# TensorE goes tile by tile instead of quad by quad: 8 units of scores, the products of the next tile, 8 blocks of rows, with one s_t buffer and score copies in twos by two engines

## The chip, the core and the metric

One Trainium2 chip; the kernel runs on one of its cores. The time is the device time of one execution in microseconds (us). Before the change it is 617.23 us (median of 3 runs, 616.33 to 617.63).

## The reference

```python
def _L0_rec_ref(F, W, K_w, Q_w):            # F (2048, 64, 128), W (64, 64, 128), K_w and Q_w (128, 128)
    Kf = jnp.einsum('bjd,ed->bje', F, K_w)
    S = jnp.einsum('bid,bjd->bij', F, Kf)   # 64 x 64 scores of each batch
    out = jnp.einsum('bij,ijd->bid', S, W)  # row i of every batch times W[i]
    out = out + jnp.einsum('bid,ed->bie', F, Q_w)
    return out
```

All in float32.

## The kernel before, in words

**Tiles, units, quads.** The 2048 batches are 16 tiles of 128. A tile is 8 units of 16 batches, a quad is 4 units, so there are 32 quads. TensorE does three kinds of work:

- *Products* (`three`, L377 to L379): F times K_w and F times Q_w, both with F transposed (128 values of d on the partitions). For accuracy F and each weight are split in a high and a low part, and a product is three matmuls with a moving operand of 512 columns (hi by hi, lo by hi, hi by lo) into one PSUM bank. A chunk is 512 columns, half a unit: one K product and one Q product, 6 matmuls. A quad has 8 chunks, 48 matmuls.
- *Scores* (`scores`, L460): for each batch a full float32 matmul with a stationary operand of 64 columns (`kf`) and a moving one of 64 (F from `f_ring`), 16 for a unit. The even and the odd batch of a pair go to the lower and the upper 64 partitions of the output, so they lie in different column halves of the array.
- *Rows* (`rows_out`, L493): for each row i of the reference a float32 matmul of W[i] (64 x 128, stationary) and the scores of that row for all 128 batches of a tile (moving, 128 columns). Row m and row 32 + m lie in different row halves of the array. A block is 4 + 4 rows, 8 matmuls, in two banks; a tile has 8 blocks, and four of them are done in each quad.

A float32 matmul of scores or rows shows in the trace as two weight loads and two matmuls, so a quad has 128 records of scores and 64 of rows.

**The other engines.** ScalarE (ACT) copies every K product out of PSUM to `kf` (`copy_kf`, L180) and every Q product to `q_out` (`copy_q`, L190), and makes the high part `f_hi` of each unit (`split_f`, L175). VectorE (DVE) makes the low part `f_lo` (L289), copies the scores of each unit from PSUM to `s_t` in three copies (`copy_s`, L315 to L317), and adds `q_out` to each block of rows (`sum_out`, L328) into one of 4 buffers of `o_sb`. SyncE (SP) issues the loads of F (1 MB for two units, into a ring of 4 such pairs) and the stores of a block (512 KB).

**Order.** Everything is written out by hand, and engines meet by semaphores. TensorE does for each quad g: the scores of g (`scores_quad`), four blocks of rows of quad r = g - 2 (`rows_quad`), the products of g + 1 (`project`). The first two quads have no rows (`project_early`), the last part is `end`. `s_t` has two buffers, one for each parity of the tile. PSUM has 8 banks; tables (STEADY, EARLY, SCORES, ROWS, END_...) say which bank is used for what, and TensorE waits before each reuse until the bank was read: for `kf_copied` and `q_copied`, `s_copied`, or `out_done`. `f_hi` and `f_lo` have a place for each of 4 units. At the start the first 8 chunks come as own loads, the first of them in two halves.

## Time and profile before

| | us |
|---|---|
| median of 3 runs | 617.23 |
| the profiled execution | 617.93 |
| its span, first to last instruction | 616.1 |
| TensorE matmuls busy | 604.9 (98%) |
| TensorE weight loads busy | 527.4 (86%) |
| VectorE busy | 460.1 (75%) |
| ScalarE busy | 391.3 (64%) |

The granted TensorE clock is 0.997 of full speed over the span. Busy times are unions of overlapping instructions, so a busy matmul row does not tell how fast the matmuls follow one another; the start times in the timeline do. The profile's page names lines of this kernel; after the change the same work has other line numbers.

### The profile page before, as it was taken

The numbers are of one execution on the slowest core, as the hardware profiler recorded it, in microseconds if no ns is written. First come the engines' busy times: TensorE is split into PE (matmuls) and PEld (weight loads), VectorE is DVE, ScalarE is ACT, GpSimd is POOL, SyncE is SP. The second block draws the span as 40 slices with busy tenths as digits, with TensorE's granted clock in tenths as the row PEclk, the third lists the DMA queues.
The fourth block names the chain that finished last, engine by engine and source line by source line (L and its number), as shares of the span: only waits on it lengthen the run. The fifth ranks groups of instructions, "written<-read, shape, count | busy, mean of one in ns | idle before, by whom it ended". The sixth has DMA issues, their size and how long they took to land.

```text
span 616.1 us, 17320 instructions
## 1 busy us (share of the span) xinstructions
PE 604.9 (98%) x7691; PEld 527.4 (86%) x7691; DVE 460.1 (75%) x647; ACT 391.3 (64%) x649; POOL 0.2 (0%) x4
## 2 busy tenths in 40 slices
PE   8999999999999999999999999999999999999994
PEld 6888888888888888888888888888888888888884
DVE  5668777787777887777887778877778777788756
ACT  7786577655677555676556775556765567765550
POOL 0000000000000000000000000000000000000000
PEclk9999999999999999999999999999999999999998
DMA  7646455775555775557755557655567655577247
GB/s 279 262 152 249 178 208 193 269 271 195 203 203 227 273 260 184 192 198 266 274 211 189 206 218 273 260 187 194 202 257 274 233 172 215 204 274 263 97 171 293
DMA packets 29161, 137.55 MB, mean 223 GB/s; under 512 B 3232, under 2 KB 3744, under 8 KB 21024
## 3 DMA queue, kind: packets, MB, share of 16 engines
q1 hardware_dynamic: 28800, 136.33, 60.0%
q8 instruction: 60, 0.98, 0.6%
q10 hardware_dynamic: 288, 0.13, 0.1%
q14 instruction: 13, 0.11, 0.0%
HBM read 69.34 MB, written 67.11 MB: 221 GB/s over the span
## 4 chain that ended last, share of the span: by engine, by line
PE 94%; DVE 3%; issue 1%; DMA 1%; ACT 1%; SPq 0%; DVEq 0%
PE ps L377 20%; PE ps L460 19%; PE ps L379 19%; PE ps L378 19%; PE ps L493 18%; DVE o_sb L328 2%; DMA f_ring<-f 1%; DVE s_t L315 0%; DVE s_t L317 0%; ACT f_hi L175 0%; DVE s_t L316 0%; DVE f_lo L289 0%; ACT q_out L190 0%; SPq L123 0%; ACT kf L180 0%
## 5 line engine op out<-in xcount | busy, mean ns | idle before, releaser
L180 ACT ACTIVATE kf<-ps 128x512 f32<-128x512 f32 x256 | 160.1, 625 | 192.9 <-PE ps L379 188.7
L289 DVE TENSOR_TENSOR f_lo<-f_ring,f_hi 128x1024 fp32r<-128x1024 f32 x124 | 146.2, 1218 | 53.3 <-ACT f_hi L175 53.2
L190 ACT ACTIVATE q_out<-ps 128x512 f32<-128x512 f32 x256 | 159.5, 628 | 5.5
L328 DVE TENSOR_TENSOR o_sb<-ps,q_out 128x1024 f32<-128x1024 f32 x128 | 150.3, 1218 | 10.3 <-PE ps L493 8.5
L460 PEld LDWEIGHTS ps<-f_ring,kf 128*64 128x64 f32 x4096 | 122.0, 138 | 11.0 <-issue 10.9
L175 ACT ACTIVATE f_hi<-f_ring 128x1024 fp32r<-128x1024 f32 x122 | 128.4, 1095 | 2.0
L460 PE MATMUL ps<-f_ring,kf 128*64 128x64 f32 x4096 | 126.5, 223 | 0.0
L493 PE MATMUL ps<-s_t,w_sb 64*128 64x128 f32 x2048 | 122.9, 275 | 1.5 <-DVE s_t L317 1.3
L493 PEld LDWEIGHTS ps<-s_t,w_sb 64*128 64x128 f32 x2048 | 116.8, 188 | 4.1 <-DVE s_t L317 1.4
L315 DVE COPY s_t<-ps 128x256 f32<-128x256 f32 x126 | 53.1, 422 | 78.5 <-PE ps L460 76.4
L377 PE MATMUL ps<-f_hi,k_hi 128*128 128x512 f32 (+1 forms) x257 | 103.5, 403 | 1.2 <-DVE f_lo L277 1.2
L379 PE MATMUL ps<-f_hi,k_lo 128*128 128x512 f32 (+1 forms) x257 | 100.2, 390 | 0.0
L378 PE MATMUL ps<-f_lo,k_hi 128*128 128x512 f32 (+1 forms) x257 | 100.0, 389 | 0.0
L377 PE MATMUL ps<-f_hi,q_hi 128*128 128x512 f32 x256 | 99.9, 390 | 0.0
L379 PE MATMUL ps<-f_hi,q_lo 128*128 128x512 f32 x256 | 99.7, 389 | 0.0
L378 PE MATMUL ps<-f_lo,q_hi 128*128 128x512 f32 x256 | 99.6, 389 | 0.0
L377 PEld LDWEIGHTS ps<-f_hi,k_hi 128*128 128x128 f32 x257 | 48.3, 188 | 14.1 <-DVE f_lo L277 1.6
L379 PEld LDWEIGHTS ps<-f_hi,k_lo 128*128 128x128 f32 x257 | 48.2, 188 | 10.3
L378 PEld LDWEIGHTS ps<-f_lo,q_hi 128*128 128x128 f32 x256 | 48.1, 188 | 10.3
L379 PEld LDWEIGHTS ps<-f_hi,q_lo 128*128 128x128 f32 x256 | 48.0, 188 | 10.4
L377 PEld LDWEIGHTS ps<-f_hi,q_hi 128*128 128x128 f32 x256 | 48.0, 188 | 10.2
L378 PEld LDWEIGHTS ps<-f_lo,k_hi 128*128 128x128 f32 x257 | 48.3, 188 | 8.8
(23 smaller groups left out, 129.7 us busy)
## 6 DMA issues: line engine op xcount, KB each, us to landing
out<-o_sb SPq DMA_DIRECT2D x128, 512.0 KB, 5.3
f_ring<-f_t SPq DMA_DIRECT2D x62, 1024.0 KB, 6.9
w_sb<-w SPq DMA_DIRECT2D x1, 2048.0 KB, 11.8
f_ring<-f SPq DMA_DIRECT2D x7, 256.0 KB, 5.2
f_ring<-f SPq DMA_DIRECT2D x2, 128.0 KB, 2.4
k_raw<-k_t ACTq DMA_DIRECT2D x1, 64.0 KB, 2.4
q_raw<-q_t ACTq DMA_DIRECT2D x1, 64.0 KB, 3.1
```

Of the source, the lines that this page charges most:

```text
L175: nc.scalar.activation(f_hi[:, e, :], f_unit(v), COPY).then_inc(fhi_done, 1)
L180: nc.scalar.activation(kf[:, c // 2, c % 2 * CK:(c % 2 + 1) * CK, :, :].rearrange("d k h i -> d (k h i)"), ps[:, product_bank(g, 2 * c), : ...
L190: nc.scalar.activation(q_out[:, t % 2, :, :].rearrange("d i (h b) -> d i h b", h=2)[:, :, :, at:at + CK], ps[:, product_bank(g, 2 * c + 1) ...
L289: nc.vector.tensor_tensor(f_lo[:, e, :], f_unit(v), f_hi[:, e, :].bitcast(F32), ALU.subtract).then_inc(flo_done, 1)
L315: nc.vector.tensor_copy(s_t[:, parity, :, same], src[:, 0, :, :])
L328: nc.vector.tensor_tensor(o_sb[:, n % OBUF, :, :], ps[:, bank:bank + 2, :], q_out[:, parity, :, :].rearrange("d (s m) b -> d s (m b)", s=2 ...
L377: nc.tensor.matmul(dst, w_hi[:, :], hi, start=True, stop=False)
L378: nc.tensor.matmul(dst, w_hi[:, :], lo, start=False, stop=False)
L379: return nc.tensor.matmul(dst, w_lo[:, :], hi, start=False, stop=True)
L460: ins = nc.tensor.matmul(ps[h * N:(h + 1) * N, score_bank(g, e), k * N:(k + 1) * N], kf[:, e, k, h, :], rows, start=True, stop=True)
L493: ins = nc.tensor.matmul(ps[:, row_bank(r, e) + s, x * P:(x + 1) * P], w_sb[half, m, :], cols, start=True, stop=True)
```

## The change

TensorE's order is by tile: the scores of tile t (8 units in 8 banks, unit e in bank e), the products of tile t + 1 (16 chunks), the 8 blocks of rows of tile t. `s_t` has one buffer, `kf` has places for 8 units, `f_hi` and `f_lo` for 3, the ring of F for 6 pairs of units. Scores leave PSUM in pairs of units (copies of 512 values for each partition instead of 256), pairs 0 and 2 by VectorE, pairs 1 and 3 by ScalarE. VectorE also makes `f_hi` of three units in a tile (`both_f`) and does its 8 sums in a row. The rows of the last tile are done in two parts (`rows_last`, `sum_last`): part 0 for the batches of units 0 to 3, part 1 for units 4 to 7, each with a moving operand of 64 columns and all 64 weights. At the start the first unit comes in four half chunks, one of them issued by ScalarE, and W is loaded right after the first 12 units of F.

```diff
-RING = 2 * UNITS // QUAD
+RING = 6
+SPLIT = 3
-        s_t = sbuf("s_t", [P, 2, HALF, P])
+        s_t = sbuf("s_t", [P, HALF, P])
...
+        def scores_of(p):
+            return ps[:, 2 * p:2 * p + 2, :].rearrange("p e (k s m) -> p s m (e k)", k=KP, s=2)
...
         @block.sync
             load_half(0)
-            load_half(1)
-            for c in range(1, CHUNKS):
+            load_half(2)
+            load_half(3)
+            for c in range(2, PIECES):
                 load_first(c)
-            load_f(2)
-            load_f(3)
...
+            for p in range(2, RING):
+                load_f(p)
+            sp.dma_start(w_sb[:, :, :].rearrange("j m d -> j (m d)"), w).then_inc(w_in, 16)
+            for t in range(TILES):
+                if t >= 1:
+                    for k in range(4, 7):
+                        store(t - 1, k)
+                load_next(t, 0)
+                if t >= 1:
+                    store(t - 1, 7)
+                for j in range(1, PAIRS):
+                    load_next(t, j)
+                for k in range(4):
+                    store(t, k)
...
         @block.scalar
+            for t in range(1, TILES):
+                copy_s(t - 1, 1)
+                copy_s(t - 1, 3)
+                for c in range(CHUNKS):
+                    copy_kf(t, c)
+                    copy_q(t, c)
+                    if c % 4 == 1:
+                        split_f(t * UNITS + 3 + c // 2)
+                split_f((t + 1) * UNITS + 2)
...
         @block.vector
+            def copy_s(t, p):
+                dve.wait_ge(s_done, t * UNITS + 2 * p + 2)
+                src, same, cross = scores_of(p), same_cols(p), cross_cols(p)
+                nc.vector.tensor_copy(s_t[:, :, same], src[:, 0, :, :])
+                nc.vector.tensor_copy(s_t[upper, :, cross], src[lower, 1, :, :])
+                nc.vector.tensor_copy(s_t[lower, :, cross], src[upper, 1, :, :]).then_inc(s_copied, 1)
...
+            for t in range(TILES):
+                v = (t + 1) * UNITS
+                copy_s(t, 0)
+                low_f(v + 2)
+                copy_s(t, 2)
+                low_f(v + 3)
+                both_f(v + 4)
+                low_f(v + 5)
+                both_f(v + 6)
+                low_f(v + 7)
+                both_f(v + 8)
+                low_f(v + 9)
+                if t < TILES - 1:
+                    for k in range(UNITS):
+                        sum_out(t, k)
+            for half in range(2):
+                for k in range(4):
+                    sum_last(half, k)
...
         @block.tensor
+            def project(t):
...
+                    if c >= 4:
+                        pe.wait_ge(kf_copied, n - 3)
+                    elif t >= 1:
+                        pe.wait_ge(s_copied_act if c % 2 else s_copied, (t - 1) * 2 + c // 2 + 1)
...
+            def scores_tile(t):
+                for e in range(UNITS):
...
+                    elif e % 2 == 0:
+                        pe.wait_ge(out_done, (t - 1) * UNITS + 5 + e // 2)
+                    scores(t, e)
+            def rows_tile(t):
+                if t == 0:
+                    pe.wait_ge(w_in, 16)
+                for k in range(UNITS):
+                    if k < 4:
+                        pe.wait_ge(kf_copied, (t + 1) * CHUNKS + 13 + k)
+                        pe.wait_ge(q_copied, (t + 1) * CHUNKS + 13 + k)
+                    else:
+                        pe.wait_ge(out_done, t * UNITS + k - 3)
+                    row_block(t, k)
+            def rows_last(part):
+                t = TILES - 1
+                for k in range(4):
...
+                    for x in range(2 * IR):
+                        m = k * 2 * IR + x
+                        for s in range(2):
+                            half = slice(s * N, (s + 1) * N)
+                            cols = s_t[half, m, :].rearrange("p (h b) -> p h b", h=2)[
+                                :, :, part * KP * 4:(part + 1) * KP * 4]
...
+                            ins = nc.tensor.matmul(ps[:, bank + s, x * N:(x + 1) * N], w_sb[half, m, :], cols,
+                                                   start=True, stop=True)
...
-            for g in range(QUADS - 1):
-                scores_quad(g)
...
-                if g >= 2:
-                    rows_quad(g)
-                    project(g + 1)
...
+            project(0)
+            for t in range(TILES):
+                scores_tile(t)
+                if t < TILES - 1:
+                    project(t + 1)
+                    rows_tile(t)
+            for part in range(2):
+                rows_last(part)
```

TensorE in the middle of the program before: the last products of a quad (L378, L379), the scores of the next (L460), rows of an earlier one (L493), the next products.

```order
L378 MATMUL ps<-f_lo,q_hi 128x512
L379 MATMUL ps<-f_hi,q_lo 128x512
L460 MATMUL ps<-f_ring,kf 64x64 x64
L493 MATMUL ps<-s_t,w_sb 128x128 x32
L377 MATMUL ps<-f_hi,k_hi 128x512
L378 MATMUL ps<-f_lo,k_hi 128x512
```

TensorE in the middle of the program now: the last products of tile t + 1 (L388, L389), the rows of tile t (L466), the scores of tile t + 1 (L440), the next products.

```order
L388 MATMUL ps<-f_lo,q_hi 128x512
L389 MATMUL ps<-f_hi,q_lo 128x512
L466 MATMUL ps<-s_t,w_sb 128x128 x64
L440 MATMUL ps<-f_ring,kf 64x64 x128
L387 MATMUL ps<-f_hi,k_hi 128x512
L388 MATMUL ps<-f_lo,k_hi 128x512
```

Runs of one kind are twice as long, and rows stand ahead of scores.

VectorE over one quad before: four score copies of three instructions each (L315 to L317), the four sums (L328) from the third on, four low parts (L289).

```order
L317 COPY s_t<-ps 64x32x8
L328 TENSOR_TENSOR o_sb<-ps,q_out 128x1024 [waits o_stored0,o_done]
L315 COPY s_t<-ps 128x32x8 [waits s_done]
L316 COPY s_t<-ps 64x32x8
L317 COPY s_t<-ps 64x32x8
L328 TENSOR_TENSOR o_sb<-ps,q_out 128x1024 [waits o_stored1,o_done]
L328 TENSOR_TENSOR o_sb<-ps,q_out 128x1024 [waits o_stored2,o_done]
L328 TENSOR_TENSOR o_sb<-ps,q_out 128x1024 [waits o_stored3,o_done]
L289 TENSOR_TENSOR f_lo<-f_ring,f_hi 128x1024 [waits fhi_done] x4
```

VectorE now, from the last low part of a tile (L292) over its eight sums (L325) to the first score copy of the next tile (L314 to L316).

```order
L292 TENSOR_TENSOR f_lo<-f_ring,f_hi 128x1024 [waits fhi_done]
L325 TENSOR_TENSOR o_sb<-ps,q_out 128x1024 [waits o_stored0,q_copied,o_done]
L325 TENSOR_TENSOR o_sb<-ps,q_out 128x1024 [waits o_stored1,o_done]
L325 TENSOR_TENSOR o_sb<-ps,q_out 128x1024 [waits o_stored2,o_done]
L325 TENSOR_TENSOR o_sb<-ps,q_out 128x1024 [waits o_stored3,o_done]
L325 TENSOR_TENSOR o_sb<-ps,q_out 128x1024 [waits o_stored0,o_done]
L325 TENSOR_TENSOR o_sb<-ps,q_out 128x1024 [waits o_stored1,o_done]
L325 TENSOR_TENSOR o_sb<-ps,q_out 128x1024 [waits o_stored2,o_done]
L325 TENSOR_TENSOR o_sb<-ps,q_out 128x1024 [waits o_stored3,o_done]
L314 COPY s_t<-ps 128x32x16 [waits s_done]
L315 COPY s_t<-ps 64x32x16
L316 COPY s_t<-ps 64x32x16
```

The sums now stand eight in a row, so the fifth waits for the store of the first of the same row of sums (o_stored0), where before a sum waited for a store of the quad before.

TensorE at the end of the program before (rows, the last four units of scores, eight blocks of rows of 128 columns):

```order
L493 MATMUL ps<-s_t,w_sb 128x128 x32
L460 MATMUL ps<-f_ring,kf 64x64 x64
L493 MATMUL ps<-s_t,w_sb 128x128 x64
```

And now (eight blocks of rows, the last eight units of scores, `rows_last`):

```order
L466 MATMUL ps<-s_t,w_sb 128x128 x64
L440 MATMUL ps<-f_ring,kf 64x64 x128
L504 MATMUL ps<-s_t,w_sb 128x64 x128
```

The last rows are 128 matmuls of 64 columns where they were 64 of 128.

## Rows read from the trace of the kernel before

**Rows 1.** The page: busy time (share of the span) and instructions of each engine.

```profile
PE 604.9 (98%) x7691; PEld 527.4 (86%) x7691; DVE 460.1 (75%) x647; ACT 391.3 (64%) x649; POOL 0.2 (0%) x4
```

**Rows 2.** TensorE's longest wait after the start: total us, times, longest.

```profile
PE ps L493 <- DVE s_t L317: 1.3, 1, 1.3
```

**Rows 3.** Timeline of PE, 318 to 338: start, us, engine, line, operation, count.

```profile
318.49 0.50 PE L377 MATMUL ps<-f_hi,k_hi 128*128 128x512 f32 x1
...
321.37 0.39 PE L377 MATMUL ps<-f_hi,k_hi 128*128 128x512 f32 x1
...
329.30 0.39 PE L379 MATMUL ps<-f_hi,q_lo 128*128 128x512 f32 x1
329.62 3.95 PE L460 MATMUL ps<-f_ring,kf 128*64 128x64 f32 x128
333.50 3.84 PE L493 MATMUL ps<-s_t,w_sb 64*128 64x128 f32 x64
337.27 0.50 PE L377 MATMUL ps<-f_hi,k_hi 128*128 128x512 f32 x1
```

**Rows 4.** Costliest groups: records | busy us, mean ns of one | idle before, releaser.

```profile
L460 PEld LDWEIGHTS ps<-f_ring,kf 128*64 128x64 f32 x4096 | 122.0, 138 | 11.0 <-issue 10.9
L493 PEld LDWEIGHTS ps<-s_t,w_sb 64*128 64x128 f32 x2048 | 116.8, 188 | 4.1 <-DVE s_t L317 1.4
```

**Rows 5.** Timeline of the end, all engines, from 592 on.

```profile
592.54 1.83 PE L493 MATMUL ps<-s_t,w_sb 64*128 64x128 f32 x28
...
593.75 1.22 DVE L328 TENSOR_TENSOR o_sb<-ps,q_out 128x1024 f32<-128x1024 f32 x1 [6.60 <-PE ps L493]
...
596.31 3.81 PEld L460 LDWEIGHTS ps<-f_ring,kf 128*64 128x64 f32 x128
596.31 3.95 PE L460 MATMUL ps<-f_ring,kf 128*64 128x64 f32 x128
...
598.28 0.41 DVE L315 COPY s_t<-ps 128x256 f32<-128x256 f32 x1
...
601.57 7.42 PE L493 MATMUL ps<-s_t,w_sb 64*128 64x128 f32 x128 [1.31 <-DVE s_t L317]
602.77 9.14 DVE L328 TENSOR_TENSOR o_sb<-ps,q_out 128x1024 f32<-128x1024 f32 x8 [1.88 <-PE ps L493]
```

**Rows 6.** Stores: the median to landing of those issued from 604.0, 611.9, 339 (two).

```profile
out<-o_sb SPq DMA_DIRECT2D x1, 512.0 KB, 2.6
out<-o_sb SPq DMA_DIRECT2D x1, 512.0 KB, 3.8
out<-o_sb SPq DMA_DIRECT2D x2, 512.0 KB, 4.7
```

**Rows 7.** The page: DMA issues: count, size, median us from issue to landing.

```profile
f_ring<-f_t SPq DMA_DIRECT2D x62, 1024.0 KB, 6.9
```

**Rows 8.** Timeline of ACT, from 325 on.

```profile
325.60 1.09 ACT L175 ACTIVATE f_hi<-f_ring 128x1024 fp32r<-128x1024 f32 x1
326.55 0.62 ACT L190 ACTIVATE q_out<-ps 128x512 f32<-128x512 f32 x1
327.02 0.64 ACT L180 ACTIVATE kf<-ps 128x512 f32<-128x512 f32 x1
```

**Rows 9.** Timeline of the start, all engines.

```profile
5.02 0.28 PE L377 MATMUL ps<-f_hi,k_hi 128*128 128x256 f32 x1
...
5.73 0.40 PE L377 MATMUL ps<-f_hi,q_hi 128*128 128x512 f32 x1
...
6.33 0.63 ACT L165 ACTIVATE f_hi<-f_ring 128x512 fp32r<-128x512 f32 x1 [1.71 <-DMA f_ring<-f]
...
7.60 0.42 DVE L283 CAST f_hi<-f_ring 128x512 fp32r<-128x512 f32 x1
...
7.74 0.50 PE L377 MATMUL ps<-f_hi,k_hi 128*128 128x512 f32 x1 [1.15 <-DVE f_lo L277]
```

More of the change, by code:

```diff
@@ L25 @@
 CK = BANK // (2 * N)
-CHUNKS = QUAD * TOK // BANK
-RING = 2 * UNITS // QUAD
+CHUNKS = UNITS * TOK // BANK
+FIRST = 4
+PIECES = FIRST * TOK // BANK
+PAIRS = UNITS // 2
+RING = 6
+SPLIT = 3
 OBUF = 4
 WARM = 8
-STEADY = (2, 3, 6, 7, 0, 1, 4, 5)
-EARLY = (6, 7, 4, 5, 0, 1, 2, 3)
-SCORES = (0, 1, 2, 3)
-ROWS = (4, 6, 0, 4)
-END_SCORES = (2, 3, 6, 7)
-END_AHEAD = (2, 6, 0, 4)
-END_ROWS = (0, 4, 2, 6)
+BOTH = [v for v in range(FIRST, TILES * UNITS) if v in (4, 5) or v >= UNITS and v % UNITS in (0, 4, 6)]
 def build(nc, f_0, f_t, k_t, q_t, w, out):
@@ L74, in build @@
         ps = psum("ps", [P, 8, BANK])
-        f_half = [sem(f"f_half{n}") for n in range(2)]
-        f_first = [sem(f"f_first{n}") for n in range(CHUNKS)]
+        f_half = [sem(f"f_half{n}") for n in range(4)]
+        f_first = [sem(f"f_first{n}") for n in range(PIECES)]
         f_in = [sem(f"f_in{n}") for n in range(RING)]
@@ new lines, in _ @@
+            sp.dma_start(w_sb[:, :, :].rearrange("j m d -> j (m d)"), w).then_inc(w_in, 16)
[10 more added lines that the diff above has]
+                    store(t, k)
+            for k in range(4, UNITS):
+                store(TILES - 1, k)
@@ L319, in sum_out, with low_f, both_f @@
-            def sum_out(r, e):
-                n = r * QUAD + e
-                u = n % UNITS
-                parity = n // UNITS % 2
+            def low_f(v):
+                if v >= TILES * UNITS:
+                    return
+                dve.wait_ge(fhi_done, sum(1 for x in range(FIRST, v + 1) if x not in BOTH))
+                low_unit(v)
+            def both_f(v):
+                if v >= TILES * UNITS:
+                    return
+                dve.wait_ge(f_in[v // 2 % RING], 16 * f_loads(v))
+                dve.wait_ge(q_done, 2 * (v - SPLIT) + 2)
+                nc.vector.tensor_copy(f_hi[:, v % SPLIT, :], f_unit(v)).then_inc(fhi_dve, 1)
+                dve.wait_ge(fhi_dve, 3 + sum(1 for x in BOTH if x <= v))
+                low_unit(v)
@@ L397, in project_first @@
                 ins.then_inc(k_done, 1)
-                pe.wait_ge(qlo_done, 1)
-                q_product(0, 0)
-                for c in range(1, CHUNKS):
-                    pe.wait_ge(flo_first, c + 2)
+            def project(t):
+                for c in range(CHUNKS):
+                    n = t * CHUNKS + c
+                    if n < 2:
+                        k_halves(n)
+                        if n == 0:
+                            pe.wait_ge(qlo_done, 1)
+                        q_product(n)
+                        continue
+                    if n < PIECES:
+                        pe.wait_ge(flo_first, n + 3)
+                    elif n % 2 == 0:
+                        pe.wait_ge(flo_done, n // 2 - FIRST + 1)
@@ L451, in scores @@
-            def scores(g, e):
-                v = g * QUAD + e
+                        pe.wait_ge(q_copied, n - 3)
+                    q_product(n)
+            def scores(t, e):
+                v = t * UNITS + e
                 for k in range(KP):
```

403 lines of the change are left out of this document (136 added, 267 removed).

## The prediction

> **What bounds the kernel now.** I read the page first: TensorE's matmuls are busy for 604.9 of 616.1 us and no other engine is above 75% [rows 1]. Then the list of waits: TensorE has almost none, the longest after the start is 1.3 us near the end [rows 2]. So time can only come out of the pace at which TensorE's own instructions follow one another, and the timeline of one quad shows that [rows 3]: products from 318.49, scores from 329.62, rows from 333.50, the next products from 337.27. That is 11.13 + 3.88 + 3.77 = 18.78 us a quad.
>
> I compare each phase with its inner pace. Products: from 321.37 to 329.30 are 35 steps, 0.2266 us each, so 48 need 10.88; the phase takes 0.25 more. Scores: a matmul is a couple of records. The 128 weight loads of a run are busy for 3.81 us [rows 5], the last of them for 0.14 [rows 4], so 63 steps from couple to couple take 3.67, 0.0583 each; 64 need 3.73, the phase takes 0.15 more. Rows: doubling a run from 64 to 128 records adds 7.42 - 3.84 = 3.58 us busy for 32 couples [rows 3, 5], 0.1119 each; the phase takes 3.77, 0.19 more than 3.58. So each quad pays 0.25 + 0.15 + 0.19 = 0.59 us for changing from one kind to the next three times.
>
> **The change part by part.** *Longer runs.* A tile has one run of each kind: scores 3.88 + 64 x 0.0583 = 7.61, products 11.13 + 10.88 = 22.01, rows 3.77 + 3.58 = 7.35, together 36.97 us, against 2 x 18.78 = 37.56. That is 0.59 less for each of 15 tiles, 8.8 us, if TensorE never waits. No matmul is added up to the last tile.
>
> *Does it wait? The sums.* I count from the start of a tile's scores: products from 7.6, rows from 29.63, next scores at 36.97. The first sum starts 1.21 after the rows (592.54 to 593.75 [rows 5]), at 30.84; eight in a row take 9.14, 1.13 from one to the next and about 1.22 for each [rows 5]. Blocks of rows come every 0.89, so the sums fall behind. Block 4 of rows (33.3) needs sum 0, over at 32.1; block 7 (36.0) needs sum 3, over at 35.5; the scores of units 0 and 1 (36.97) need sum 4, over at 36.6; units 2, 4 and 6 (38.8, 40.7, 42.6) need the sums that end at 37.7, 38.8 and 40.0. No wait, but only 0.4 to spare at two places. The sums have to start on time: the last low part on VectorE before them depends on ScalarE's split after chunk 13 (28.6) and ends at about 29.8, 1.0 early.
>
> *The stores.* There are 4 output buffers, so sum 4 (35.4) waits for store 0, issued at 32.1. A store without other traffic lands in 2.6 us, the eighth of eight in a row in 3.8 [rows 6]: 34.7. Sum 7 (38.8) needs store 3, about 38.6. SP issues the loads of F in between: the first stands behind the stores of blocks 4 to 6 and goes out at 2.3 instead of 2.1, the last at 7.8. At a median of 6.9 us to landing [rows 7] they are over long before 32, so I take the values without traffic. Stores issued some us after two loads took 4.7 [rows 6]. The F that the first load brings is split from 13.4 on, 11 us after its issue.
>
> *Score copies.* A copy of 512 values from PSUM is in no row. Bounds: 0.42 (256 values [rows 5]) and 1.13 (the sum of 1024 [rows 5]); on the line between, 0.66. VectorE's copy of pair 0 goes from 3.0 to 5.0, a low part to 6.1, pair 2 to 8.1. The products' chunk 0 wants pair 0 at 7.6 and chunk 2 wants pair 2 at 10.4. With 1.13 a copy they end at 6.4 and 10.9: 0.5 late. ScalarE takes 0.47 for 512 values and 0.95 for 1024 in a row [rows 8], so pair 3 goes from 7.8 to 9.3 and the first kf copy (ready at 8.6) starts 0.7 late. A product comes every 0.68, ScalarE wins 0.2 on each and loses 0.95 with a split; TensorE allows it four chunks, 5.4 us. Hidden.
>
> *Three places for f_hi and f_lo.* Unit v + 3 of a tile can be split when the products of unit v are done (10.7). ScalarE splits it after two copies, 11.2 to 12.2, the low part (1.13) is there at 13.5, and TensorE wants it at 15.9: 2.4 to spare. Units v + 5 and v + 7 repeat this; v + 4 and v + 6, both parts by VectorE, have 3. VectorE's work in a tile gets less: 6 copies of 0.66 for 24 of 0.42, plus three high parts of about 0.7 (estimated from the copies).
>
> *The start.* TensorE waits from 6.42 to 7.74 for chunk 1, whose 256 KB ScalarE gets at 6.33 [rows 9]. As two halves, the first issued earlier, it should be there about one microsecond sooner, but chunk 2 is no earlier: VectorE got it at 7.60 [rows 9], and TensorE now asks for its split at 7.8. Bounds of the waiting that is left: 0 and 1.3; I take 0.5. Then scores start at 5.02 + 2 x (0.71 + 0.68) + 14 x 1.36 + 0.09 + 0.5 = 27.4 (0.71 is a K product in halves, 5.02 to 5.73).
>
> *The last rows.* `rows_last` has 128 matmuls of 64 columns where 64 of 128 did, with twice the weight loads. Is a couple of rows paced by its moving columns or by its weights? Rows (128 stationary, 128 moving) take 0.1119, scores (64 and 64) 0.0583: both explain that. The weight-load records are 188 ns for 128 stationary columns and 138 for 64 [rows 4]: 50 ns for 64 columns, so the streaming part for 128 is at least 100 ns, all of the pace of rows. I therefore take 0.1119 for a couple also with 64 moving columns: 128 x 0.1119 = 14.32 us. The lower bound is 128 x 0.0583 = 7.5; above 14.3 there is none, since two loads of that width already pass in that time together with twice the moving columns.
>
> The Trainium skill ("TensorE: Matmul & The Clock Gate", section LDWEIGHTS) says that a weight load takes its columns divided by 1.2 ns, whatever the rows: an estimate of 107 ns for 128 columns. The same page's section on the back-to-back gap has a rule by moving columns alone. By the first rule the last rows would take 13.7 us, by the second they would be at the lower bound; the slope of the weight-load rows agrees with the first. It speaks against this part of the change.
>
> **The sum.** Scores of tile 0 at 27.4; plus 15 x 36.97 = 554.6 gives 582.0 for the scores of the last tile, plus 7.6 gives 589.6 for the last rows (their score copies come in time: pairs 0 and 1 by 5.9, pair 3 at 9.3, before block 3). Last sum: 14.32 + 0.32 later (0.32 is 1.21 less 8 couples), 604.3; 1.21 for it, 0.03 to issue, 2.6 to land, and 0.4 from the last landing to the end as before (611.9 + 3.8 to 616.1 [rows 6]): 608.5. That is 7.6 under the span of 616.1, so 610.3 for an execution like the profiled one (617.9), and 617.2 - 7.6 = **609.6 us** for the median.
>
> **Rivals.** *A, the forecast*: last rows at the pace of weights, no wait in the tiles, 609.6.
>
> *B, last rows at the pace of moving columns.* Then the eight sums bound the end: 589.6 + 0.93 + 0.32 + 7 x 1.13 + 1.21 + 0.03 + 3.8 + 0.4 = 604.2, 4.3 less: 605.3. For it: scores with 64 moving columns do run at half the time. Against it: they have half the stationary columns too.
>
> *C, small waits in each tile*, where 0.4 is to spare: a sum chain or a PSUM copy later than I walked it. At 0.3 for each of 15 tiles, 4.5 more: 614.1. For it: two margins of 0.4, and no row for the 512 copy. Against it: the paces are steady to hundredths.
>
> *D, slower: sums wait for stores.* If a store lands in 4.7 us, as after loads [rows 6], store 0 lands at 36.8, sum 4 ends at 38.0 and TensorE waits 1.0 before units 0 and 1: 15 x 1.0 = 15 more, 625. It decides from the landing of store 0: above 3.7 us TensorE waits, above 4.2 the 0.5 a tile that was to be gained is gone. Against it: no load is issued within 24 us ahead.
>
> *E, the change doesn't do what it says*: the 0.59 is not paid for changing kind, but comes for each 4 units, as from instruction supply. Then a tile still takes 37.56, 8.8 more: 618.4. Against it: inside a run the steps are even.
>
> **Chances.** A 0.57, B 0.17, C 0.15, D 0.07, E 0.04. A measurement of this kernel can tell about 0.2% (1.2 us) from no change. Faster: A, B and most of C, 0.88; within 0.2%: 0.04, out of C; slower: D, most of E, 0.08. The range takes in B and most of C: 604.6 to 614.3, with D, E and the worse part of C left out.
>
> **What would show it.** In the profile after: scores, products and rows of a tile at 7.61, 22.01 and 7.35 us with a period of 36.97; if a phase is longer, the list of waits names sum, copy or store. Couples of the last rows 0.11 apart (A) or 0.06 (B). Sum 4 of each tile with no idle time ahead (not D). TensorE's wait for chunk 1 under 0.5 us. I am wrong if TensorE shows waits in each tile, or if the gap at a change of kind grows with the length of the run.

## The result and the profile after

The kernel after takes 621.12 us (median of 6 runs, 618.88 to 623.89), against 617.19 for the kernel before, timed beside it (6 runs): 1.0065 times as long, with a 95% interval of 1.0049 to 1.0082. The forecast was 609.6 with a range to 614.3: wrong in sign. The profiled execution took 620.9 us, its span is 619.1, and the granted TensorE clock is 0.995 of full speed over the span.

The page of the kernel after: busy engines, the queue of instructions, and the issues of stores and loads with their median to landing (these answer to [rows 1] and [rows 7]):

```profile
PE 606.5 (98%) x7822; PEld 535.9 (87%) x7822; DVE 403.9 (65%) x411; ACT 402.0 (65%) x695; POOL 0.2 (0%) x4
...
q8 instruction: 62, 1.02, 0.6%
...
out<-o_sb SPq DMA_DIRECT2D x128, 512.0 KB, 4.4
f_ring<-f_t SPq DMA_DIRECT2D x62, 1024.0 KB, 10.5
```

Two things are new. A load lands in 10.5 us where it took 6.9 [rows 7]. And there is a queue that I had not looked at: the engines' own instructions come by DMA during the run, in 62 packets, 1.02 MB in all, 16 KB each.

Next the timeline of TensorE's matmuls over one tile (start, us, engine, line, operation, count):

```profile
139.14 7.68 PE L440 MATMUL ps<-f_ring,kf 128*64 128x64 f32 x256
146.75 0.50 PE L387 MATMUL ps<-f_hi,k_hi 128*128 128x512 f32 x1
...
168.76 7.42 PE L466 MATMUL ps<-s_t,w_sb 64*128 64x128 f32 x128
176.10 0.57 PE L440 MATMUL ps<-f_ring,kf 128*64 128x64 f32 x12
```

Scores 7.61, products 22.01, rows 7.34, a tile 36.96: what was forecast, to a hundredth. Other tiles are longer. The list of waits (engine, line, releaser: total, times, longest) has them, where [rows 2] had one of 1.3 us:

```profile
DVE o_sb L325 <- DMA out<-o_sb: 11.1, 10, 1.8
...
PEld ps L388 <- issue: 2.9, 1, 2.9
...
PEld ps L440 <- issue: 2.3, 5, 0.6
...
PEld ps L387 <- issue: 2.1, 1, 2.1
...
PEld ps L440 <- DVE o_sb L325: 0.9, 3, 0.4
```

The rows named PEld are TensorE's weight loads; the matmul behind a late load waits with it. Most of TensorE's new waits end with "issue": no engine and no data transfer of the program released it. Timeline of matmuls at the longest:

```profile
258.89 0.39 PE L388 MATMUL ps<-f_lo,q_hi 128*128 128x512 f32 x1
259.12 0.39 PE L389 MATMUL ps<-f_hi,q_lo 128*128 128x512 f32 x1
262.23 0.39 PE L387 MATMUL ps<-f_hi,k_hi 128*128 128x512 f32 x1 [2.72 <-issue]
```

And the same stretch by windows (busy time of each engine, then granted clock, DMA share, GB/s): the DMA engines are full all the while.

```profile
259.00:260.00 1.00, 0.51 (x3) 0.27 (x2) 0.00 (x0) 0.96 (x3) 0.00 (x0) 1.00 0.98 385
260.00:261.00 1.00, 0.00 (x0) 0.00 (x0) 0.00 (x0) 0.88 (x2) 0.00 (x0) 1.00 1.06 434
261.00:262.00 1.00, 0.00 (x0) 0.00 (x0) 0.00 (x0) 0.00 (x0) 0.00 (x0) 1.00 0.99 414
```

Among those transfers, between 259.75 and 260.8, is one packet of the queue of instructions:

```profile
q8 instruction: 1, 0.02, 5.6%
```

The second long wait, matmuls again:

```profile
448.64 0.40 PE L387 MATMUL ps<-f_hi,k_hi 128*128 128x512 f32 x1
448.88 0.39 PE L388 MATMUL ps<-f_lo,k_hi 128*128 128x512 f32 x1
451.14 0.39 PE L389 MATMUL ps<-f_hi,k_lo 128*128 128x512 f32 x1 [1.87 <-issue]
...
452.66 0.63 PE L389 MATMUL ps<-f_hi,k_lo 128*128 128x512 f32 x1
...
455.22 0.63 PE L389 MATMUL ps<-f_hi,k_lo 128*128 128x512 f32 x1
455.65 0.46 PE L387 MATMUL ps<-f_hi,q_hi 128*128 128x512 f32 x1
```

This one settles what kind of wait it is. It lies inside one product, between the lo by hi and the hi by lo matmul, where the code has no semaphore at all. It costs 2.0 us. From 1.2 us after its end on, steps of 0.43 in place of 0.23 follow, 1.6 us more.

Where the 10.6 us go that lie between forecast and trace at the end (608.5 and 619.1): I took the start times of all matmuls and subtracted the steady steps. After the first score:

| what | us |
|---|---|
| eight waits ended by "issue": 0.40, 0.42, 0.06, 2.88, 0.65, 0.16, 2.03, 0.61 | 7.2 |
| the slow steps after the wait at 448.88 | 1.6 |
| four small waits at the first or second unit of scores of a tile (0.15 to 0.25) | 0.8 |
| steps of under 0.05 each | 0.7 |
| start (27.24 for 27.4) and end (27.0 from the last scores for 26.5) | 0.3 |

All eight waits of the first line come at the same place in TensorE's stream: counting all its instructions in the trace (weight loads, matmuls and the 198 semaphore and drain instructions among them, 15,842 in all), 193 or 194 past a multiple of 256. And 62 packets of 16 KB for 15,842 instructions are 64 bytes each, 256 to a packet. So the waits lie where a new block of instructions begins.

The packets confirm it. Packet n (the first is 0) can be laid beside instruction 256(n + 1) + 193. At the eight waits TensorE goes on 1.20 to 1.54 us after that packet has landed: the one from 259.79 to 260.72 stands ahead of the restart at 262.23, the one from 448.93 to 449.89 ahead of 451.14. In the kernel before, laid out in the same way, every packet lands at least 2.7 us ahead of its place.

The end, answering to [rows 5]: last rows, weight loads and matmuls.

```profile
599.73 14.37 PEld L504 LDWEIGHTS ps<-s_t,w_sb 64*128 64x128 f32 x256
599.73 14.51 PE L504 MATMUL ps<-s_t,w_sb 64*128 64x64 f32 x256
```

### The profile page after: what moved, and what is told of

Read it like the earlier page. It is cut to its first block, busy times and chain, and to the rows that moved or that the text cites. A ratio compares the mean times of both kernels' runs of the same rounds, so it can differ in the third digit from the quotient of the medians.

```text
span 619.1 us, 17442 instructions
## 1 busy us (share of the span) xinstructions
PE 606.5 (98%) x7822; PEld 535.9 (87%) x7822; DVE 403.9 (65%) x411; ACT 402.0 (65%) x695; POOL 0.2 (0%) x4
## 3 DMA queue, kind: packets, MB, share of 16 engines
q8 instruction: 62, 1.02, 0.6%
## 4 chain that ended last, share of the span: by engine, by line
PE 94%; DMA 2%; DVE 1%; issue 1%; ACT 0%; DVEq 0%
PE ps L440 20%; PE ps L387 19%; PE ps L389 19%; PE ps L388 19%; PE ps L466 15%; PE ps L504 2%; DMA out<-o_sb 2%; DVE o_sb L325 1%; PE ps L511 1%; DVE o_sb L338 0%; ACT s_t L219 0%; ACT s_t L217 0%; DVE zeros L345 0%; ACT s_t L218 0%; DVEq L91 0%
## 5 line engine op out<-in xcount | busy, mean ns | idle before, releaser
L292 DVE TENSOR_TENSOR f_lo<-f_ring,f_hi 128x1024 fp32r<-128x1024 f32 x124 | 151.8, 1224 | 163.5 <-ACT f_hi L194 161.9
L208 ACT ACTIVATE q_out<-ps 128x512 f32<-128x512 f32 x256 | 156.7, 612 | 7.5 <-PE ps L389 0.3
L325 DVE TENSOR_TENSOR o_sb<-ps,q_out 128x1024 f32<-128x1024 f32 x120 | 140.2, 1219 | 32.5 <-PE ps L466 20.7
L199 ACT ACTIVATE kf<-ps 128x512 f32<-128x512 f32 x256 | 155.6, 608 | 7.8 <-PE ps L389 4.3
L217 ACT ACTIVATE s_t<-ps 128x512 f32<-128x512 f32 x32 | 19.1, 598 | 180.7 <-PE ps L440 180.7
L440 PE MATMUL ps<-f_ring,kf 128*64 128x64 f32 x4096 | 125.0, 223 | 1.7 <-issue 1.4
L440 PEld LDWEIGHTS ps<-f_ring,kf 128*64 128x64 f32 x4096 | 121.8, 138 | 5.0 <-issue 2.3
L466 PEld LDWEIGHTS ps<-s_t,w_sb 64*128 64x128 f32 x1920 | 108.4, 188 | 5.3 <-issue 5.3
L466 PE MATMUL ps<-s_t,w_sb 64*128 64x128 f32 x1920 | 111.2, 274 | 0.0
L387 PE MATMUL ps<-f_hi,k_hi 128*128 128x512 f32 (+1 forms) x258 | 102.0, 395 | 2.7 <-issue 2.7
L389 PE MATMUL ps<-f_hi,k_lo 128*128 128x512 f32 (+1 forms) x258 | 100.5, 390 | 1.9 <-issue 1.9
L388 PE MATMUL ps<-f_lo,k_hi 128*128 128x512 f32 (+1 forms) x258 | 100.5, 389 | 0.0
L389 PE MATMUL ps<-f_hi,q_lo 128*128 128x512 f32 x256 | 99.9, 390 | 0.0
L388 PE MATMUL ps<-f_lo,q_hi 128*128 128x512 f32 x256 | 99.9, 390 | 0.0
L194 ACT ACTIVATE f_hi<-f_ring 128x1024 fp32r<-128x1024 f32 x77 | 82.0, 1064 | 0.0
L388 PEld LDWEIGHTS ps<-f_lo,k_hi 128*128 128x128 f32 x258 | 48.7, 189 | 12.5 <-issue 2.9
L387 PEld LDWEIGHTS ps<-f_hi,k_hi 128*128 128x128 f32 x258 | 48.7, 189 | 10.6
L389 PEld LDWEIGHTS ps<-f_hi,k_lo 128*128 128x128 f32 x258 | 48.6, 189 | 10.1
L388 PEld LDWEIGHTS ps<-f_lo,q_hi 128*128 128x128 f32 x256 | 48.3, 189 | 10.1
L389 PEld LDWEIGHTS ps<-f_hi,q_lo 128*128 128x128 f32 x256 | 48.2, 188 | 10.2
## 6 DMA issues: line engine op xcount, KB each, us to landing
f_ring<-f_t SPq DMA_DIRECT2D x62, 1024.0 KB, 10.5
```

Source lines behind the costliest of these rows:

```text
L194: nc.scalar.activation(f_hi[:, v % SPLIT, :], f_unit(v), COPY).then_inc(fhi_done, 1)
L199: nc.scalar.activation(kf[:, c // 2, c % 2 * CK:(c % 2 + 1) * CK, :, :].rearrange("d k h i -> d (k h i)"), ps[:, 2 * c % 8, :], COPY).then ...
L208: nc.scalar.activation(q_out[:, t % 2, :, :].rearrange("d i (h b) -> d i h b", h=2)[:, :, :, at:at + CK], ps[:, (2 * c + 1) % 8, :].rearra ...
L217: nc.scalar.activation(s_t[:, :, same], src[:, 0, :, :], COPY)
L292: nc.vector.tensor_tensor(f_lo[:, v % SPLIT, :], f_unit(v), f_hi[:, v % SPLIT, :].bitcast(F32), ALU.subtract).then_inc(flo_done, 1)
L325: nc.vector.tensor_tensor(o_sb[:, n % OBUF, :, :], ps[:, bank:bank + 2, :], q_out[:, t % 2, :, :].rearrange("d (s m) b -> d s (m b)", s=2) ...
```

## The experiments

The theory (F in some of the expectations): TensorE's next block of instructions comes late, because its DMA runs behind data that the DMA engines already have. A block lasts 3.8 us in scores (512 records take 7.61) and 7.3 in rows, but a load takes about 10 us to land. The rivals: the sums and their stores hold TensorE up; or the waits belong to the work at that place; or long fast stretches need instructions faster than they come, whatever the data traffic (L in the first expectations; in that of late_stores, L says that the four loads alone are enough).

| kernel | median us (lowest to highest, runs) | ratio to before (95%) | span of the profile |
|---|---|---|---|
| light_loads | 616.73 (614.60 to 619.17, 10) | 0.9982 (0.9968 to 0.9997) | 615.2 |
| light_stores | 612.68 (612.60 to 613.36, 4) | 0.9925 (0.9909 to 0.9942) | 610.9 |
| spaced_loads | 616.81 (615.66 to 617.85, 10) | 0.9986 (0.9976 to 0.9995) | 615.7 |
| wide_end | 620.77 (618.41 to 624.68, 7) | 1.0068 (1.0037 to 1.0100) | 617.2 |
| quiet_scores | 613.71 (613.45 to 613.99, 5) | 0.9936 (0.9923 to 0.9948) | 611.9 |
| quiet_wide | 612.06 (611.07 to 613.45, 5) | 0.9912 (0.9898 to 0.9927) | 611.6 |
| shifted | 624.75 (1) | | 622.9 |
| before_traffic | 621.93 (621.55 to 622.94, 4) | 1.0074 (1.0059 to 1.0090) | 619.8 |
| late_stores | 622.37 (617.99 to 628.08, 10) | 1.0059 (1.0034 to 1.0084) | 626.3 |
| quiet_buf5 | 611.81 (611.36 to 614.16, 6) | 0.9916 (0.9904 to 0.9929) | 609.6 |
| split_loads | 618.83 (616.29 to 621.40, 10) | 1.0018 (1.0002 to 1.0034) | 617.4 |
| split_both | 664.47 (664.08 to 665.94, 4) | 1.0766 (1.0750 to 1.0782) | 663.0 |

**light_loads.** All loads of F after the first six pairs bring an eighth of the bytes; the rest of each pair keeps old values, and the instructions stay.

```diff
-                             f_t[p, :, :]).then_inc(f_in[p % RING], 16)
+                cols = 2 * TOK if p < RING else 2 * TOK // 8
+                ... f_t[p, :, :cols]).then_inc(f_in[p % RING], 16)
```

> The changed kernel, but after the first 12 units each load of F brings only 256 of its 2048 columns (128 KB instead of 1 MB), so later products and scores use old F. Theory F (TensorE's program comes by DMA in blocks of 256 instructions, and a block is late when the DMA engines have a backlog of loads and stores while scores and rows use up a block in 3.8 us): the gaps inside scores and products at positions 193 or 194 modulo 256 of TensorE's instructions vanish, every tile takes 36.97 us, the time is 609 to 611 us. Theory L (the run of rows and scores, now 768 instructions in 15 us, outruns the supply of instructions by itself, whatever the data traffic): the gaps stay, 619 to 622 us.

616.73: below the kernel after and hardly below before, between what F (609 to 611) and L (619 to 622) asked. The two long waits and the slow steps are gone. Short ones stay, in the middle of scores, in its list of waits:

```profile
PEld ps L441 <- issue: 3.0, 7, 0.7
```

So the long waits need the full loads, and the short ones don't; loads alone are not the whole cause.

**light_stores.** Each store writes 64 KB in place of 512; the rest of the output is not written.

```diff
-                sp.dma_start(out[t, k, :, :], ...
+                sp.dma_start(out[t, k, :, :IR * P // 4], ...[:, :IR * P // 4] ...
```

> The changed kernel, but each store writes only 256 of the 1024 columns of its block (128 KB instead of 512 KB). Theory F: the stores are the backlog at the beginning of the scores, so most gaps at the block boundaries go; those behind the burst of four loads (late in the scores, early in the products) may stay; no sum waits for a store; 609 to 615 us. Theory L: the gaps stay and only the sums' waits of about 1 us in all go, 618 to 621 us.

612.68. (The edit writes 64 KB a store, not the 128 of the expectation.) The first two tiles of its trace take 1.1 us more each, with a wait at a block boundary in either; from the third on a tile takes 36.97, but for one that takes 0.6 and one that takes 0.1 more. The loads are untouched, and nearly all later waits are gone, the long ones too. Each cure removes more than its own part, as if it counted how much data is in line when the block of instructions is asked for; late_stores, below, shows that this is not the whole of it.

**spaced_loads.** All bytes, but load j of a tile also waits for a K product (2j + 1) of the next tile, so the four loads are spread over the products.

```diff
                     sp.wait_ge(s_done, t * UNITS + 2 * j + 2)
+                    sp.wait_ge(k_done, (t + 1) * CHUNKS + 2 * j + 1)
```

> The changed kernel, complete, but SP issues the four loads of F of a tile one by one during the products: load j waits in addition for the K product of chunk 2j of the next tile, so no load is under way during rows and scores. Theory F: nearly no gaps at block boundaries, 609 to 613 us; the F of the first load lands about 1 to 2 us before its split, so no new wait for F. Theory L: 619 to 622 us. If F comes late instead, VectorE and then TensorE wait in the products at unit 4 of each tile, some 0.5 us a tile more.

616.81, as light_loads, and again between F (609 to 613) and L (619 to 622): no long wait, but some 3 us of short ones in the scores, where the stores still are.

**quiet_scores.** SyncE issues the four loads and the stores of blocks 4 to 7 only during the products, in turn, so that nothing is issued while scores run. Same instructions on all other engines.

```diff
-                    for k in range(4, 7): store(t - 1, k)
-                load_next(t, 0)
-                ...
+                for j in range(PAIRS):
+                    in_products(t, 3 * j)          # waits k_done
+                    load_next(t, j)
+                    if t >= 1:
+                        in_products(t, 3 * j + 2)
+                        store(t - 1, 4 + j)
```

> The changed kernel, complete, with another order on SP alone: during the products of a tile, paced by waits for K products of chunks 0 to 11, it issues load 0, store 4, load 1, store 5, load 2, store 6, load 3, store 7; stores 0 to 3 go out as before. So nothing but the rest of stores 0 to 3 is under way during the scores. Theory F (late instruction blocks, because of the backlog of data DMAs): the gaps at 193 and 194 modulo 256 in scores and early products go, and as loads and stores no longer meet, no sum waits for a store: tiles at 36.97 us, 609.5 to 611.5 us. Theory L (the long run by itself): 616 us or more, as with spaced loads.

613.71: 7.4 us under the kernel after with the same work and the same bytes. At the block boundaries 0.12 us of waiting is left in the trace after the first tile. This is the clearest run: TensorE's long fast stretch does no harm by itself. It is still 2 us over what F asked (609.5 to 611.5): the expectation had no sum waiting for a store, and its trace has 2.0 us of TensorE waiting for such sums.

**late_stores.** Only the stores of blocks 4 to 7 go into the products; the loads stay in the scores.

```diff
+                for j in range(PAIRS): load_next(t, j)
+                for k in range(4, UNITS):
+                    sp.wait_ge(k_done, (t + 1) * CHUNKS + 3 * k - 9)
+                    store(t - 1, k)
```

> The kernel after, with one edit: SyncE issues the stores of blocks 4 to 7 of the tile before not in the first microseconds of the scores but one by one during the products (after 3, 6, 9 and 12 K products). The four loads are issued at their old places, during the scores. Theory S (TensorE's next instructions come late only where a backlog of data transfers and a long fast stretch meet; the stores of the tile before are the first half of that backlog, as light_stores had it with lighter stores): the waits of 0.2 to 0.8 us in the middle of the scores go, the two large waits in the early products go as well or stay single, span 611 to 612.5, median 612.5 to 614. Rival L (the burst of four loads alone is enough for the large waits): the two waits of 2 to 3 us near 259 and 449 us, with the slow clock behind one of them, stay or come at other tiles, span 615 or more. Rival N (instruction supply has nothing to do with it): as the kernel after, 619 to 621.

622.37, no better than the kernel after: theory S there fell, rival L held. The profile is of the longest of its ten runs, so I take places from it and no totals. TensorE in one tile (scores begin at 178.76):

```profile
181.27 4.53 PE L439 MATMUL ps<-f_ring,kf 128*64 128x64 f32 x147 [0.42 <-DVE o_sb L324]
187.70 1.50 PE L439 MATMUL ps<-f_ring,kf 128*64 128x64 f32 x44 [1.91 <-issue]
```

DMA queues of that kernel from 178.8 to 185.1 (packets, MB, share): only data.

```profile
q1 hardware_dynamic: 291, 1.64, 69.8%
issues: line engine op xcount, KB each, median us to landing
f_ring<-f_t SPq DMA_DIRECT2D x2, 1024.0 KB, 5.6
```

And from 185.1 to 187.6: the block of instructions, just ahead of TensorE's restart.

```profile
q8 instruction: 1, 0.02, 2.2%
```

In light_stores, where the first load was issued at nearly the same point of the scores (2.3 us into them, here 2.1), the block of this tile (scores from 178.08) came at 181.3 to 182.4, in a stretch in which the DMA engines had moments of rest, and the scores ran through:

```profile
178.08 7.68 PE L441 MATMUL ps<-f_ring,kf 128*64 128x64 f32 x256
...
185.70 0.50 PE L388 MATMUL ps<-f_hi,k_hi 128*128 128x512 f32 x1
```

```profile
q8 instruction: 1, 0.02, 5.3%
```

The block is either just ahead of the loads or behind them. That heavier stores push the block before it back, and so this one behind the loads, fits both traces, but it is argued, not shown. The spread of this kernel (10 us over ten runs) would go with such a race.

**before_traffic.** The reverse, in the kernel before: one more load of 1 MB for each quad, into a spare buffer that nobody reads, issued after the first unit of scores.

```diff
+                if g < QUADS:
+                    sp.wait_ge(s_done, g * QUAD + 1)
+                    sp.dma_start(spare[:, :], f_t[g, :, :]).then_inc(spare_in, 16)
```

> The kernel before, with one more load of 1 MB in each quad into a spare place that nobody reads, issued when the first unit of scores is done, ahead of the two loads of F. Theory F: the kernel before too gets gaps at one residue modulo 256, in scores, rows or the first products, and takes 619 to 630 us; its sums may wait for stores as well. Theory L: its runs are short, so no such gaps, at most waits of sums, 617 to 619 us.

621.93, slower by what theory F in its bare form would ask, but not for its reason. The quads keep their pace, as in [rows 3]:

```profile
328.83 3.95 PE L467 MATMUL ps<-f_ring,kf 128*64 128x64 f32 x128
332.72 3.84 PE L500 MATMUL ps<-s_t,w_sb 64*128 64x128 f32 x64
336.49 0.50 PE L384 MATMUL ps<-f_hi,k_hi 128*128 128x512 f32 x1
```

317.71 to 336.49 is 18.78. The loss is at the end. SyncE issues the last added load ahead of four stores, so these go out from 597.10 on, where before it was 595.00, and take 9.8 us to land, where it was 4.7; a sum waits for the first of them, and TensorE for the sum:

```profile
DVE o_sb L335 <- DMA out<-o_sb: 4.4, 1, 4.4
PEld ps L500 <- DVE o_sb L335: 3.3, 3, 1.5
```

Its packets of instructions all land at least 3.1 us ahead of their places. So traffic does no harm either with short fast stretches (scores and rows of a quad are 384 records in 7.65 us, between products that need 11.1 us for 96). With quiet_scores this says that both are needed: a long stretch (768 records in 15 us) and data in line.

**shifted.** Are the waits tied to the block or to the work at that place? 32 small matmuls ahead of the first product (64 records) move all block boundaries against the work.

```diff
+            for n in range(32):
+                nc.tensor.matmul(ps[:, 0, :N], zeros[:, :P], zeros[:, :N], start=True, stop=True)
             pe.wait_ge(klo_done, 1)
```

> The changed kernel with 32 more small matmuls of zeros (64 records of TensorE) ahead of the first product, about 2 us. If late blocks of 256 instructions cause the gaps (F), they stay at the same residue, 193 or 194 modulo 256 counted over all of TensorE's records, and so move to other places of the work: the gap inside the scores of a tile moves 32 couples earlier. If they belong to a place of the work (a wait for another engine), they stay at the same couple of the same tiles and their residue moves by 64. 617 to 626 us.

In the kernel after the third tile (scores from 101.67) waits at 106.33, 4.66 us into them. Now:

```profile
110.32 7.68 PE L440 MATMUL ps<-f_ring,kf 128*64 128x64 f32 x255
119.09 0.27 PE L440 MATMUL ps<-f_ring,kf 128*64 128x64 f32 x1 [1.09 <-issue]
```

The wait is after record 510 of 512. 64 records are 0.95 us of scores, so the old boundary is now at 3.7 and the next, 3.8 on, at 7.5: there. All of its "issue" waits at scores and products are again at 193 or 194 of 256. They belong to the block. In this trace and the ten others of the kernel after and its variants but split_both, each of the 45 steps of over 0.3 us at such a place ends 1.2 to 1.6 us after a packet of instructions has landed. (My expectation took a batch of scores for two records; it is four, with its weight loads.) The single time of 624.75 is no price of the waits: the 32 matmuls took 6.9 us and not 2, the lower clock was granted until 17.2 us where it was 5.2, and the first scores start at 36.2 for 27.2. From there to its last scores this trace is 5.4 us shorter than that of the kernel after.

**wide_end.** The last rows as the tiles have them: 64 matmuls of 128 columns.

```diff
-            for part in range(2):
-                rows_last(part)
+            pe.wait_ge(s_copied, TILES * 2)
+            pe.wait_ge(s_copied_act, TILES * 2)
+            rows_tile(TILES - 1)
```

> The changed kernel, but the rows of the last tile are done as those of all others, 64 matmuls of 128 columns, after all score copies, and not in two parts. If the last rows are paced by their weight loads (theory W: 128 x 0.112 us with 64 columns), the rows start 1.8 us later, take 7.2 instead of 14.5 us, and eight sums at 1.13 us bound the end: 24 us from the last scores to the end instead of 27, so 2.5 to 3.5 us less than the changed kernel, near 618 us. If the end was bound by something else, no difference.

Matmuls, then VectorE, of its end (last scores from 591.45):

```profile
601.19 7.42 PE L462 MATMUL ps<-s_t,w_sb 64*128 64x128 f32 x128 [1.99 <-ACT s_t L219]
```

```profile
602.39 7.15 DVE L325 TENSOR_TENSOR o_sb<-ps,q_out 128x1024 f32<-128x1024 f32 x6 [1.84 <-PE ps L462]
610.77 2.46 DVE L325 TENSOR_TENSOR o_sb<-ps,q_out 128x1024 f32<-128x1024 f32 x2 [1.23 <-DMA out<-o_sb]
```

Half the records take half the time: 14.51 / 256 and 7.42 / 128 are 0.057 and 0.058 us each, with 64 columns moving and with 128. The pace is that of the weights. But only 1.2 of the 7.1 us come through (25.8 from last scores to the end, against 27.0): the rows start 2.1 later, since they want all score copies, and the sums then wait for stores. The median is not told from that of the kernel after, and the 618 expected did not come.

**quiet_wide.** quiet_scores and wide_end together.

> As quiet_scores, and the rows of the last tile as 64 matmuls of 128 columns. By theory F 1.2 us less than quiet_scores (the tail with wide rows took 25.8 us from the last scores against 27.0): 608.5 to 610.5 us. By theory L near 615 us.

612.06: faster than both kernels, but 1.6 us over the range expected. What is left in its trace over 36.97 a tile is 2.1 us, 1.8 of it at the first or second unit of scores. The wide end gave nothing in it: from the last scores to the end it took 26.8 us, in quiet_scores 26.7. TensorE waits 2.0 us for the last score copy, then the granted clock is at the lower level from 595.6 to 599.0, and the last rows take 9.04 us where wide_end had 7.42.

**quiet_buf5.** One more buffer of sums, 5 in place of 4. The raw weights share its place until its first use, and 19 warm-up matmuls of 216 columns stand for 8 of 512.

```diff
-OBUF = 4
+OBUF = 5
...
+        k_raw = o_sb[:, OBUF - 1, 1, :D]
+        q_raw = o_sb[:, OBUF - 1, 1, D:2 * D]
```

> quiet_wide with one more buffer for the sums: 5 places of o_sb in place of 4 (to make room, the raw weights lie in the fifth place until its first use, and the warm-up matmuls have 216 columns in place of 512, 19 of them in place of 8). The sum of block 4 then no longer waits for the store of block 0 of its own tile. Theory W (what is left over 36.97 us a tile in quiet_wide, about 1.8 us in all, and the tail are sums that wait for stores to land, which hold PSUM banks and so TensorE): these waits go, every tile takes 36.97, the tail is up to 1 us shorter, since its sums wait for a store later; span 609 to 610, median 610 to 611, against 612.1 for quiet_wide. Rival V (these waits come from elsewhere, as from the DMA that fetches VectorE's or ScalarE's instructions): span as quiet_wide, 611.6, and gaps of 0.3 to 0.6 us at the first scores or the second unit stay.

Waits in quiet_wide:

```profile
DVE o_sb L327 <- DMA out<-o_sb: 15.3, 12, 2.2
...
PEld ps L438 <- DVE o_sb L327: 2.0, 5, 0.5
```

and in quiet_buf5, where TensorE has none on a sum:

```profile
DVE o_sb L327 <- DMA out<-o_sb: 1.6, 5, 0.5
```

All 15 tiles take 36.97, and the scores of the last begin at 582.58, where the forecast had 582.0. So theory W is right on the waits. On the time it is not shown: the profile of quiet_wide is of its slowest execution and that of quiet_buf5 of its fastest, so the 2.0 us between their spans say nothing. The median of 611.81 is above the 610 to 611 expected and is not told from quiet_wide (the intervals of the two ratios nearly coincide). The last rows took 9.04 us here too, with the lower clock from 594.2 to 597.6.

**split_loads and split_both.** Does the block wait for one transfer or for all in line? Each 1 MB load as four of 256 KB, and in split_both each store as four too.

```diff
+                for x in range(4):
+                    cols = slice(x * TOK // 2, (x + 1) * TOK // 2)
+                    sp.dma_start(f_ring[...][:, cols], f_t[p, :, cols]).then_inc(f_in[p % RING], 16)
```

> The kernel after, with each 1 MB load of F issued as four loads of 256 KB (a quarter of the columns each, 2 KB for a partition instead of 8), at the same place: same bytes, same time of day, smaller pieces. Both theories hold that TensorE's next 16 KB of instructions come late behind data transfers; they differ in what it waits for. Theory P (it waits for the rest of one transfer's share on its DMA engine, 2.5 us for 1 MB, 0.6 for 256 KB): the waits of 2 to 3 us in the early products and those behind loads go or fall under 0.4; those behind stores (512 KB, 1.3 us) stay; span 613 to 616, median 615 to 618. Rival Q (it waits for all that is queued ahead, whatever its pieces): as the kernel after, with a wait of 2 to 3 us near 259 or 449, span 618 to 621. The Trainium skill (DMA: Bandwidth & Descriptors, Queues, rings and completion order) states that a DMA engine goes round its queues and changes between them only at the end of a packet of descriptors; P would be that rule with the share of one transfer as the packet.

618.83, with a span of 617.4, between the spans that P (613 to 616) and Q (618 to 621) asked. The largest wait of the weight loads fell from 2.9 us to

```profile
PEld ps L390 <- issue: 1.3, 1, 1.3
```

where P asked for under 0.4 and Q for 2 to 3, and 5.4 us of waits at block boundaries remain (7.2 in the kernel after). Neither holds as it stands. By the Trainium skill ("DMA: Bandwidth & Descriptors", section Queues, rings and completion order) a DMA engine changes between queues only at the end of a packet of descriptors. The trace of late_stores is not against it, but does not show when the block was asked for (data from about 182 on, the block at 185.19, a little over the 2.5 us that 1 MB takes at some 400 GB/s, an estimate); split_loads does not bear out that a quarter of the piece is a quarter of the wait. What exactly stands ahead of the block stays open.

> As split_loads, and each 512 KB store also issued as four of 128 KB (1 KB for a partition). Theory P: no wait of TensorE for instructions over 0.2 us is left after the first 80 us, except where the clock fell; what remains are sums that wait for a store (0.8 to 2 us in all); span 611 to 613, median 613 to 615. Rival Q: as the kernel after, span 618 to 621. Against both: if the smaller pieces cost the DMA engines more than a tenth of their rate, stores land later, and DVE waits for them longer than 11 us in all.

It tells nothing on that, since it has a new bound. Timeline of SyncE's queue:

```profile
305.78 14.24 SPq L153 DMA_DIRECT2D out<-o_sb  x22
320.06 1.89 SPq L138 DMA_DIRECT2D f_ring<-f_t  x4
```

An issue takes SyncE 0.47 us here (1.89 / 4). Stores go out late, VectorE waits for them 68.0 us in all and TensorE for VectorE 37.1, in its list of waits:

```profile
DVE o_sb L330 <- DMA out<-o_sb: 68.0, 51, 2.9
...
PEld ps L445 <- DVE o_sb L330: 37.1, 25, 2.2
```

## Why the prediction was wrong

**Longer runs: right.** Phases 7.61, 22.01, 7.34 and period 36.96, as worked out. The 0.59 us for changing kind three times is real, and rival E (instruction supply as a cost for each 4 units) did not happen.

**"If TensorE never waits", the step that failed.** The 8.8 us were there to be had: all 15 tiles of quiet_buf5 take 36.97 in its trace, though its median is only 5.8 us below that of the kernel before, beside it. I looked for waits on semaphores only. Traffic was weighed for the sums ("I take the values without traffic", "they are over long before 32") and for nothing else. I never asked what the loads and stores in the first 12 us of a tile do to TensorE itself. They delay its instructions by 7.2 us, and 1.6 come on top while the granted clock was at the lower of its two levels, 1.2 GHz for 2.4 (steps of 0.43 for 0.23). Two parts of the change make this together: a fast stretch of rows and scores that is twice as long, and eight stores followed by four loads just there, where before two loads and four stores fell to each 18.78 us. I named instruction supply in rival E, at 0.04, with the wrong mechanism; with the right one it would have been a slower case, as it was. The rest of the miss is small: the sum left out 0.8 us of waits for sums, 0.7 of small steps and 0.3 at start and end.

**Sums and stores: right in place, wrong in "no wait".** The margins of 0.4 us were those that gave. VectorE waited for a store to land 10 times, 11.1 us in all; nearly all of it lies in slack, and TensorE lost 0.8 us, at the units where I had 0.4 to spare (2 us in quiet_scores). This is C at a fifth of its price, by D's mechanism, in four tiles of 15. "Against it: no load is issued within 24 us ahead" missed what else can be in line. Why the late tiles come five apart is not settled: in the trace of `shifted` they came one tile later, which points to the block of instructions again, met by a store.

**Score copies, three places of f_hi: right.** A copy of 512 values took 0.69 us on VectorE and 0.60 on ScalarE (0.66 taken). No wait follows from either.

**Start: right.** First scores at 27.24 for 27.4.

**Last rows: right in kind.** 14.51 us for 14.32; A over B: with 128 stationary columns a couple takes 0.113 us, with 64 moving columns as with 128. The working was partly luck: it took one streaming part of 100 ns for a couple, which has two weight loads. The estimate of 13.7 from the Trainium skill's rule for weight loads ("TensorE: Matmul & The Clock Gate", section LDWEIGHTS) counts one load for a couple too. For 256 loads one after the other the rule gives 27 us, an estimate as well. They took 14.5, since loads overlap in the trace: one takes 188 ns [rows 4] and they start 57 ns apart. The same page's rule by moving columns alone does not hold for these rows.

**The chances.** They don't add up as told: A, B and the rest of C behind the 0.04 give 0.85 for faster, not 0.88, and D with E 0.11, not 0.08. Either way slower was held unlikely, and none of it was for what came. A range that ended at 614.3 rested on the idea that every cost had a row in the trace before; this one had a row on the page (60 packets of instructions in the kernel before) that I did not read.

## What to carry to other kernels

Count an engine's instructions against its time. In this program 256 records of scores go by in 3.8 us, and a load took 6.9 us and more to land: where an engine gets through a block of instructions faster than the data in line are moved, schedule the loads and stores into its slow stretches, at no cost in bytes or work (7.4 us here). When joining short runs of small instructions into long ones, ask what transfers fall in the new run, and read the page's rows on the instruction queue. A wait marked "issue", in the middle of an accumulation with no semaphore, is the sign.

## What the runs showed of the hardware that I had not expected

- TensorE's stream of 15,842 instructions comes with 62 packets of 16 KB on a queue of its own; waits for it fell at one place, 193 to 195 of 256 instructions, in all variants of the kernel after, the shifted one too, and ended 1.2 to 1.6 us after a packet had landed.
- Such a wait is up to 2.9 us, and the slow steps came after the shorter one of the two: granted clock 1.00 after 2.9 us without a matmul at 259, and 0.67 over 451 to 455 after 2.0 us at 449. In late_stores it fell after the waits that ended at 227.4 and 419.4 (2.0 and 2.2 us) and not after that at 187.7 (2.1 us). Windows of the kernel after:

```profile
263.00:266.00 3.00, 3.00 (x15) 2.49 (x14) 0.64 (x1) 2.81 (x5) 0.00 (x0) 1.00 1.00 421
```

```profile
451.00:455.00 4.00, 3.86 (x12) 3.06 (x12) 1.16 (x1) 3.02 (x5) 0.00 (x0) 0.67 1.02 429
```

- Issuing a DMA from SyncE takes 0.47 us where many go out in a row in split_both, and 0.33 us for a store by itself in the kernel before (at 604.02). The 48 issues for each tile in split_both are 22.6 us of its queue, with stores behind loads in it, and the kernel is 43 us slower than the kernel after.
